# Maxima in full tiles of 128 rows, queries projected turned for teams of batches, score stacks of three terms, and all queues in a new order

## What is computed

```python
# layer 0: 32 query heads, 8 key heads, head size 16; B, L, S = 16, 100, 361
q = x @ Wq + bq; k = ctx @ Wk + bk; v = ctx @ Wv + bv
scores = einsum('bkgld,bksd->bkgls', q, k) / sqrt(16) + mask
out = einsum('bkgls,bksd->bkgld', softmax(scores), v) @ Wo + bo
x = layernorm(out + x) * gamma + beta
# layer 1: one head of size 512
scores = (x @ w_q.T) @ (ctx @ w_k.T).T / sqrt(512)
x = x + alpha * ((softmax(scores) @ (ctx @ w_v.T)) @ w_o.T)
```

## Time and profile before

| what | value |
|---|---|
| time, median of 3 runs | 671.33 us (668.79 to 672.84) |
| the profiled execution, first to last instruction | 672.3 us |
| TensorE matmuls busy | 643.7 us (96%) |
| VectorE busy | 494.6 us (74%) |
| ScalarE, GpSimd busy | 396.1 us, 397.9 us (59% each) |
| mean granted TensorE clock | 0.992 of full |
| DMA | 110.93 MB in 47355 packets |

### The profile page before, as it was taken

How to read it: one execution, slowest core, us unless ns; L and a number is a source line. 1 busy time by engine, 2 the same in 40 slices (tenths; PEclk the granted TensorE clock), 3 DMA queues, 4 the chain that set the end, 5 groups by cost and what they waited for, 6 DMA issues and landing times.

```text
span 672.3 us, 11851 instructions
## 1 busy us (share of the span) xinstructions
PE 643.7 (96%) x3756; PEld 472.5 (70%) x3756; DVE 494.6 (74%) x1453; ACT 396.1 (59%) x588; POOL 397.9 (59%) x254
## 2 busy tenths in 40 slices
PE   3999899999999999999999999999999999999887
PEld 2656567777767878777777778787777777756454
DVE  2259488887778787878787878878787888785742
ACT  3314477766657666756766676766566656665321
POOL 7344568766465766667665657576666567563220
PEclk9999799999999999999999999999999999999999
DMA  8687564765574766767474747667675755443212
GB/s 290 226 185 213 127 174 136 194 187 126 145 238 110 229 155 195 165 183 194 137 215 128 238 106 240 135 200 172 189 175 158 203 138 151 121 101 117 88 45 71
DMA packets 47355, 110.93 MB, mean 165 GB/s; under 512 B 10095, under 2 KB 31663, under 8 KB 46783
## 3 DMA queue, kind: packets, MB, share of 16 engines
q1 hardware_dynamic: 47294, 110.19, 59.4%
HBM read 87.29 MB, written 22.46 MB: 163 GB/s over the span
## 4 chain that ended last, share of the span: by engine, by line
PE 75%; DMA 9%; issue 5%; POOL 4%; SPq 2%; DVE 2%; ACT 2%; POOLq 0%; DVEq 0%; ACTq 0%
PE mx_ps L750 11%; PE work L709 10%; PE work L710 10%; PE work L711 10%; PE o_ps L766 8%; PE work L823 6%; PE work L874 5%; PE sc_ps L737 3%; PE sc_ps L730 3%; PE sc_ps L738 3%; DMA qs<-mt_l 3%; PE work L779 3%; POOL pr L3948 2%; DMA k_dr<-k_l 2%; DMA qs<-q_dr 2%
## 5 line engine op out<-in xcount | busy, mean ns | idle before, releaser
L2406 DVE CUSTOM_DVE_ANT_0 mx_ps<-mx_ps,mask_n 100x361 f32<-100x361 f32 x512 | 271.6, 543 | 70.6 <-PE mx_ps L750 65.7
L3948 POOL TENSOR_TENSOR pr<-pr,mask_t 128x800 f32<-128x800 f32 x124 | 236.8, 1917 | 76.3 <-ACT pr L3252 75.9
L750 PE MATMUL mx_ps<-ks,qs 96*100 96x362 f32 x512 | 181.9, 369 | 0.9 <-DMA qs<-q_dr 0.6
L3259 ACT ACTIVATE pr<-pr 128x1200 f32<-128x1200 f32 x128 | 149.5, 1206 | 9.4 <-POOL pr L3948 5.4
L3252 ACT ACTIVATE pr<-sc_ps 128x800 f32<-128x800 f32 x124 | 104.0, 839 | 77.8 <-PE o_ps L766 51.0
L750 PEld LDWEIGHTS mx_ps<-ks,qs 96*100 96x100 f32 x512 | 84.4, 166 | 39.0 <-DVE mx L2406 11.3
L2392 DVE TENSOR_TENSOR pr<-sc_ps,mask_t 128x400 f32<-128x400 f32 x124 | 70.9, 572 | 24.6 <-PE sc_ps L730 14.3
L3960 POOL TENSOR_TENSOR c_l<-cT,c_h 128x1448 fp32r<-128x1448 f32 x16 | 53.4, 3338 | 51.4 <-ACT c_h L3284 51.4
L766 PE MATMUL o_ps<-pr,va 128*32 128x400 f32 (+1 forms) x768 | 73.0, 514 | 0.0
L2406 DVE DVE_READ_ACCUMULATOR2_ANT mx<- 100x1 f32 x512 | 72.3, 141 | 0.0
L823 PEld LDWEIGHTS work<-late 128*128 128x128 f32 (+1 forms) x384 | 49.7, 191 | 7.0 <-issue 5.9
(11 more groups left out here) (163 smaller groups left out, 1223.4 us busy)
## 6 DMA issues: line engine op xcount, KB each, us to landing
qs<-q_dr SPq DMA_DIRECT2D x64, 200.0 KB, 4.3
ks<-k_dr SPq DMA_DIRECT2D x128, 96.0 KB, 3.7
late<-in_ctx SPq DMA_DIRECT2D x16, 768.0 KB, 7.2
cT<-in_ctxT SPq DMA_DIRECT2D x16, 724.0 KB, 5.4
late<-in_ctxT SPq DMA_DIRECT2D x16, 724.0 KB, 6.0
o_dr<-o_s SPq DMA_DIRECT2D x30, 200.0 KB, 3.5
xT<-in_xT SPq DMA_DIRECT2D x16, 200.0 KB, 3.9
q_dr<-q_h SPq DMA_DIRECT2D x16, 200.0 KB
```

Source lines behind the costliest of these rows:

```text
L750: nc.tensor.matmul(mx_ps[0:L, n % 2, 0:SP2], qs[p][0:TERMS, g, L * j:L * (j + 1)], ks[p][0:TERMS, g, 0:SP2], start=True, stop=True).then_i ...
L2406: V.tensor_tensor_reduce(out=src, in0=src, in1=mask_n[p][:, :], scale=1.0, scalar=-3.0e38, op0=ALU.add, op1=ALU.max, accum_out=mx[p][:, n: ...
L3259: A.activation(t, t, ACT.Exp).then_inc(ex_ok, 1)
L3948: G.tensor_tensor(t, t, mask_t[p][:, 1:3, :].unsqueeze(2).to_broadcast([P, 2, J, L]), ALU.add).then_inc(sc_pool, 1)
```

## The change

- **Maxima.** `heads` becomes `tiles`: the 400 query columns of each key head (4 heads x 100) are cut into three tiles of 128 columns; the 16 left over of each of the 8 key heads make one more tile of 8 x 16 = 128, gathered by `rests` on GpSimd into `rest` and computed by four accumulating matmuls. That is 25 tiles of 128 rows (28 matmuls) for 32 of 100 rows. The mask has to follow the cut: `mask_n` holds four orders of the rows (128 x 4 x 361, one buffer), loaded by three DMAs `mask_in(b, c)`. `rests(b)` waits for the queries of both halves.
- **Maxima back.** Turned maxima are 13 rows of 128; `maxima_in` needs eight DMAs per half (three of 4 x 128 and one of 4 x 16 elements, for high and low) for two.
- **Queries.** `q_part(t, j, k0, k1)` works for a team of two or three batches: Wq is now the weights, 128 columns of it at a time, and the x columns of the whole team (200 or 300) move. The result comes out turned; `turn_q`, `q_natural` and the broadcast bias are gone; the bias is added in `q_high` and `q_low`. A team takes 48 matmuls of 300 (or 200) columns for 12 of 512 per batch.
- **Stacks.** The low x low term is dropped from scores and maxima. `ks` holds two key heads per slot (rows 0 to 47 and 48 to 95, each high, high, low), `qs` holds a head's three terms in its 48 rows and zeros in the others. `keys_in` and `queries_in` take the place of `stacks_in`, four DMAs each per half. `k_dr` and `q_dr` have a place for every batch, so writing no longer waits for reading.
- **Order.** The lists of all engines are new; the 36 matmuls that nobody reads are gone. Layer 0's projection of the first batch begins with keys and values.

The diff, cut to its core (the call lists are thousands of lines):

```diff
+PAIRS = KVH // 2
+REST = JL - SC * P
+TILES = KVH * SC + 1
+HALF_TILES = (KVH // 2) * SC + 1
+TEAMS = ((0, 1), (2, 3, 4), (5, 6, 7), (8, 9, 10), (11, 12, 13), (14, 15))
+def tile_of(n):
+    if n == HALF_TILES - 1:
+        return SC, None
+    m = n if n < HALF_TILES else n - HALF_TILES
+    return m // 4, m % 4 + (0 if n < HALF_TILES else 4)
...
-            def stacks_in(b, half, r0, r1):
...
+            def keys_in(b, half):
+                p, ps = b % 2, slice(2 * half, 2 * half + 2)
+                sp.wait_ge(k_out[p], 32 * (b // 2 + 1))
+                wait(sp, s0_mm, 8 * (b - 2) + 4 * half + 4)
+                wait(sp, s1_mm, 8 * (b - 2) + 4 * half + 4)
+                for t in range(2):
+                    r0 = TERMS // 2 * t
+                    src = k_dr[b, 0, :, t, ps, :].rearrange("d g s -> d (g s)").unsqueeze(0)
+                    sp.dma_start(ks[p][r0:r0 + 2 * HD, ps, :].bitcast(F32).rearrange("r g s -> r (g s)"),
+                                 src.to_broadcast([2, HD, 2 * SC * P])).then_inc(st_in[half][p], 16)
+                    sp.dma_start(ks[p][r0 + 2 * HD:r0 + 3 * HD, ps, :].bitcast(F32),
+                                 k_dr[b, 1, :, t, ps, :]).then_inc(st_in[half][p], 16)
...
             def maxima_in(b, half):
...
-                for row, t in ((TERMS, mt_h[half]), (TERMS + 1, mt_l[half])):
-                    dst = qs[p][row:row + 1, 4 * half:4 * half + 4, :].bitcast(F32).rearrange(
-                        "p g (j l) -> p (g j) l", j=J)
-                    sp.dma_start(dst, t[:, :].bitcast(F32)).then_inc(m_in[half], 16)
+                    for c in range(SC):
+                        dst = qs[p][row:row + 1, gs, P * c:P * (c + 1)].bitcast(F32)
+                        src = t[first + 4 * c:first + 4 * c + 4, :].bitcast(F32)
+                        sp.dma_start(dst, src).then_inc(m_in[half], 16)
+                    dst = qs[p][row:row + 1, gs, SC * P:JL].bitcast(F32)
+                    sp.dma_start(dst, t[last:last + 1, 64 * half:64 * half + 64].bitcast(F32)).then_inc(m_in[half], 16)
...
-            def heads(b, n0, n1):
...
+            def tiles(b, n0, n1):
+                p = b % 2
+                for n in range(n0, n1):
+                    c, g = tile_of(n)
+                    at = TILES * b + n
+                    if n == 0:
+                        pe.wait_ge(st_in[0][p], 128 * (b // 2 + 1))
+                    if n == HALF_TILES - 1:
+                        pe.wait_ge(rest_ok, b + 1)
+                    wait(pe, a_mx, at - 1)
+                    dst = mx_ps[:, at % 2, 0:SP2]
+                    if g is None:
+                        for r in range(PAIRS):
+                            w = 96 * (r + 1)
+                            mm = nc.tensor.matmul(dst, rest_flat[:, w:w + P], ks[p][0:TERMS, r, 0:SP2],
+                                                  start=(r == 0), stop=(r == PAIRS - 1))
+                    else:
+                        mm = nc.tensor.matmul(dst, qs[p][0:TERMS, g, P * c:P * (c + 1)], ks[p][0:TERMS, g // 2, 0:SP2],
+                                              start=True, stop=True)
+                    mm.then_inc(a_mm, 1)
...
-            def q_part(b, k0, k1):
+            def q_part(t, j, k0, k1):
+                n = len(TEAMS[t])
...
-                    mm = product(work[0:L, 1, :], x_h[:, xs], x_l[:, xs], wq_h[:, k, :], wq_l[:, k, :], k, KT - 1)
+                    mm = product(work[:, 1, 0:n * L], wq_h[:, k, js], wq_l[:, k, js],
+                                 x_h[:, k, 0:n, :].rearrange("p i l -> p (i l)"),
+                                 x_l[:, k, 0:n, :].rearrange("p i l -> p (i l)"), k, KT - 1)
...
-            def fill_scores(b, g, c, count):
...
-            def keep_busy(count, free, value):
...
+            def rests(b):
+                p = b % 2
+                for half in range(2):
+                    pool.wait_ge(st_in[half][p], 128 * (b // 2 + 1))
+                wait(pool, a_mm, TILES * (b - 1) + HALF_TILES if b else 0)
+                G.tensor_copy(rest[:, :, 96:P].rearrange("k r (t i) -> k r t i", t=2),
```

More of the change, by code:

```diff
@@ L951, in pack_rows @@
                                  start=(half == 0), stop=(half == 1)).then_inc(g_mm2[half], 1)
-            def fill_scores(b, g, c, count):
-                pe.wait_ge(*((sc_add, 8 * b + g) if c == 0 else (sc_cp, 8 * b + g)))
-                for _ in range(count):
-                    nc.tensor.matmul(sc_ps[0:L, 2 if c else 0, :], wk_h[:, 0, 0:L], wq_h[:, 0, :], start=True, stop=True)
-            def fill_first(count):
-                for _ in range(count):
-                    nc.tensor.matmul(mx_ps[0:L, 1, :], wk_h[:, 0, 0:L], wq_h[:, 0, :], start=True, stop=True)
@@ L962, in keep_busy @@
-            def keep_busy(count, free, value):
-                pe.wait_ge(free, value)
-                dst = sc_ps[0:L, 2, :] if free is fl_ok and value == 3 else o_ps[0:L, :]
-                for _ in range(count):
-                    nc.tensor.matmul(dst, wk_h[:, 0, 0:L], wq_h[:, 0, :], start=True, stop=True)
-            q_part(0, 0, 4)
-            fold_m(0, 0, 1)
-            turn_q(0)
-            fold_m(2, 0, 1)
-            fold_m(3, 0, 1)
-            k_part(0, 0, 3)
-            fold_m(1, 0, 1)
@@ new lines, in _ @@
+            scores(2, 3, 1, 3)
+            tiles(3, 6, 7)
+            scores(2, 2, 0, 1)
+            q_part(2, 0, 0, 2)
+            turn_x1(0)
+            tiles(3, 7, 8)
+            q_part(2, 0, 2, 4)
+            tiles(3, 8, 9)
+            scores(2, 4, 1, 3)
+            scores(2, 3, 0, 1)
+            tiles(3, 9, 10)
+            xm_part(0, 0, 1)
+            tiles(3, 10, 11)
+            xm_part(0, 1, 4)
+            tiles(3, 11, 12)
+            scores(2, 4, 0, 1)
+            tiles(3, 12, 13)
@@ L1266, in _ @@
+            tiles(4, 2, 3)
+            turn_x1(1)
+            scores(3, 3, 1, 3)
+            tiles(4, 3, 5)
+            turn_maxima(3, 1)
+            xm_part(1, 0, 2)
+            scores(3, 3, 0, 1)
+            tiles(4, 5, 6)
             xm_part(1, 2, 3)
-            heads(3, 31, 32)
+            tiles(4, 6, 7)
             xm_part(1, 3, 4)
-            scores(3, 1, 0, 1)
-            scores(3, 3, 1, 3)
-            turn_maxima(3, 1)
+            tiles(4, 7, 8)
+            k_part(5, 0, 1)
@@ new lines, in _ @@
+            k_part(9, 1, 2)
+            tiles(8, 5, 6)
+            scores(7, 3, 0, 1)
+            k_part(9, 2, 3)
+            tiles(8, 6, 7)
+            s1_part(5, 0, 4)
+            scores(7, 4, 1, 3)
+            tiles(8, 7, 8)
+            scores(7, 4, 0, 1)
+            values(7, 0)
+            turn_p1(5)
+            k_part(9, 3, 4)
+            tiles(8, 8, 10)
+            scores(7, 5, 0, 1)
+            cx_part(5, 0, 2)
+            tiles(8, 10, 11)
+            scores(7, 5, 1, 3)
@@ new lines, in _ @@
+            tiles(11, 6, 7)
+            scores(10, 4, 1, 3)
+            cx_part(8, 0, 2)
+            scores(10, 5, 0, 1)
+            tiles(11, 7, 8)
+            scores(10, 5, 1, 3)
+            tiles(11, 8, 9)
+            cx_part(8, 2, 4)
+            tiles(11, 9, 10)
+            k_part(12, 2, 3)
+            scores(10, 6, 0, 1)
+            tiles(11, 10, 11)
+            scores(10, 6, 1, 3)
+            k_part(12, 3, 4)
+            d_part(8, 0, 1)
+            tiles(11, 11, 12)
+            d_part(8, 1, 3)
```

3885 lines of the change are left out of this document (1793 added, 2092 removed).

## The result

The changed kernel takes **780.22 us** (median of 4 runs, 777.93 to 781.58), the kernel before 671.02 us on the same chip: a ratio of 1.162, 95% interval 1.158 to 1.165. The forecast was 634 us, faster. It is slower by 109 us. One execution of all that follow, of `before_nofill` (681.32 us), fell in a slower state of the chip and is left out.

A forecast was written before the change was run, and what follows sets the result against it. TensorE was taken to bound the kernel, streaming 95% of the time in steady state. The terms sum to -37 us against 672.3, giving 635 for that execution and a forecast of 634 us, range for 8 in 10 613 to 660.

The forecast's parts named there:

- Terms 1 to 3: TensorE: 28 maxima matmuls for 32, -10.6 us; queries in 300 or 200 columns, -8 us; 64 query turns gone, -5.6 us.
- Term 7: SP and DMA engines: 10 us more issuing per batch, 26.5 us in all, taken as hidden, cost 0.
- term 6: Maxima's way back to the scores: eight issues, 0.25 us wait per half, +8 us (bounds 0, +35); +2 us at the end.
- Term 5: VectorE: fewer maxima and no bias addition, so TensorE waits less: -9 and -9 us (bounds 0 and -30).
- term 4: TensorE: the 36 unread matmuls, fillers where it waited, are gone: -5 us (bounds 0 and -13).
- The start: Early batches begin with smaller weights, but the first matmul waits for GpSimd's low part either way: 0.
- Term 8: GpSimd: the copy `rests`, one per batch, costs 0 while the stacks land half a batch ahead.
- SP becomes the bound: Rival, SP's list: waits stay in series with 26.5 us of issuing, period 37.2 us, 682 us; chance 0.06.
- The clock: Rival, TensorE: without unread matmuls more stretches at half clock follow the first batches' waits, +12 us, 646 us; chance 0.08.

The follow-up runs named there:

- before_nofill: Kernel before without its 36 unread matmuls: 670.3 us, ratio 1.000.
- keys_first: Changed kernel with 15 `keys_in` calls that stand closely behind a `maxima_in` moved ahead of it in SP's list: 771.7 us, ratio 1.149.
- none_start: Changed kernel without maxima DMAs, its first 30 us rearranged (first queries' low part ahead of second context's, Wo's splits behind those of the queries): 709.67 us.
- none_norest: Changed kernel without maxima DMAs, tile 12 computed from the first half's stacks, waiting neither for the gathering copy nor the second half's stacks: 700.63 us.
- before_split: Kernel before with each half's maxima carried in eight DMAs of 4 x 100 elements for two of 16 x 100: 740.47 us, ratio 1.104.
- before_none: Kernel before without any DMA of the maxima, a constant -25 in their place: 665.57 us, ratio 0.993.

## Why the prediction was wrong

**Read rightly:** that TensorE bounded the kernel before, and every pace. Terms 1 to 3 are in the trace (28 matmuls at the pace of 362 columns, 300 columns in 0.14 us, no turns), and so is the streaming, 31 us less where these terms and the 8.4 us of unread matmuls make 32.6. SP's 26.5 us of issuing a batch and its 0.59 us an issue came as reckoned.

**Term 7 is the step that failed**, "Hidden in my forecast, cost 0", and with it **term 6**, +8 us between bounds of 0 and +35. Together eight issues cost 78 us over none in the new order, and 70 over two in the old. Term 6 was reckoned as the way of one half, 7.4 us needed and 7.3 there. It left out that the list goes on behind the eight issues: the stacks of the next batch come 5.0 us later than without them, the tiles with them, and the next maxima start late. The loss of one half is the start of the next. I had written that SP has these stacks "ahead of them", from the one place that I showed; in the chain above the keys stand behind. And the cover was set against the landing of 1.8 us; landings on the path took 2.3 to 4.5 us for the maxima and 6 to 6.7 us for the keys. How much of the 78 us is each half's own wait and how much the delay of what stands behind, no run separates: `keys_first` turned one into the other.

**Term 5**, -18 us for VectorE's relief, did not come. VectorE is relieved (57%), and in the steady state the period is 36.9 us with or without it, once the issues are away. Of **term 4**, the -5 us are not there: taken from the kernel before alone, the unread matmuls change the time by less than 3 us either way.

**The start** was put at 0, "the first matmul waits for GpSimd's low part either way". That matmul is 0.4 us later (11.2 for 10.8 us), but the first maximum is 18.5 us later, and `none_start` shows that such a delay reaches batch 15 whole. I followed the first matmul, where the chain to the first tile (keys, values, folds, 48 query matmuls for two batches, each split in turn) had to be followed. Together with 16 us in batches 0 to 4, whose cause no run looked for, this is most of the offset of 37 to 45 us.

**Term 8**, cost 0, holds by `none_norest` within the scatter, although the waits of the changed kernel name the copy with 10.7 us; the masks in term 7 were hidden as said.

**The rivals.** "SP becomes the bound" had the right mechanism and too small a size: I let it decide "once more than 10.3 us of waits per batch stay in the series". With a period of 42.3 us and 26.5 of issuing, 15.8 us of them stayed. Its 682 us also took its price only in the steady state. I held against it that SP's waits were it being early; but its wait for the split of the maxima did not shrink, 75.6 to 85.3 us; as I read it, being late with one thing made it wait for the next. In the old order the argument held in part: in `before_split` that wait fell to 60.2 us. "The clock": it fell, to 0.87 where I had named the first quarter, and without the 36 unread matmuls: but these are not what held it up, since `before_nofill` has 0.995. It falls with the issues (0.973 with none in the new order, 0.921 with eight; 0.992 and 0.962 with two and eight in the old), so it follows the waits. Its own share of the 109 us stays open; the four executions speak for a small one. The chance of 0.07 for slower was too small: rows showed a queue in strict order with single waits of up to 8.7 us, its load was reckoned at 77%, and I summed the savings and only listed the risk.

**By the sum:** 780 less 634 is 146 us. The way of the maxima is 78 us for 10 forecast, 68. The offset of the new order at no issues is 37. The other 41 are what 624 us, my forecast without term 6 (634 - 10), lies below `before_none` (666): savings that never arrived. That the three parts add up says nothing for them: the last is what is left.

**Still open** is what holds the new order at 36.9 us a batch with no maxima carried, though it streams 2 us less. Masks and the gathered tile are excluded by runs as causes of more than a few us. The chain there goes through the reciprocals' way over DRAM and the keys' stacks behind them in SP's list; that was read, not tried. That the old order has the same period (36.9 us) where TensorE fills it may be chance.

## What to carry to other kernels

Where one engine issues every DMA in order, cost a new issue by what stands behind it in the list, as well as by its own wait: here it was nothing that could be measured for the 45 issues of the mask, and 0.25 to 0.43 us each for those of the maxima, once there were more than two or four a half, on a path that comes round in every batch. Before cutting one transfer into several, try just that in the kernel as it is; here one small edit would have told 70 of the 109 us. And follow a pipeline's fill up to the first instruction of its slowest stage: the one delay measured there, 7.3 us, was still there at the last batch.

## What the runs showed of the hardware

- An issue of a DMA of 4 x 128 elements took SP 0.58 us in the median, one of 4 x 16 elements 0.59 us, as much as one of 16 x 100 before: cutting a transfer makes no piece cheaper to issue. The Trainium skill, DMA: Bandwidth & Descriptors, section Anatomy of one DMA, gives some 50 ns for the sequencer's dispatch, but on the path of DMAs that GpSimd issues; it is no price for SP's issues here, nearly all of which take 0.3 to 0.8 us.
- The work can't be handed away for free: from ScalarE's queue the same issues took 0.63 us each and showed up as 40 us of waits for ScalarE's results.
- The landing of a small DMA is no constant: 2.3, 4.5 and 7.6 us for the maxima at different places of the changed kernels, beside 1.7 at least before. By the same section a DMA issued by GpSimd has a fixed cost of about 2 us; no run here has one, and SP's shortest landings of the maxima lie near that figure, those on the path between it and almost four times as much.
- Waits named by the profile need not be worth anything: those for the gathered tile went from 7.1 us to 0 and the time by 1.6 us, inside the scatter.
- Half the clock does not mean an idle engine: in the changed kernel's stretches at 1.2 GHz matmuls are busy for 106 of 123 us, and two executions with mean clocks of 0.890 and 0.932 took 779.9 and 781.6 us.
